# All expert pairs' gated rows split in a high and a low part, normalisations moved to ScalarE, the weights' low parts made on VectorE

## Time and profile before

| | |
|---|---|
| Median of 3 runs | 746.45 us |
| The profiled execution's own time | 748.99 us |
| Its span, first to last instruction | 746.8 us |
| PE busy | 689.9 us (92%), 2943 instructions |
| PE weight loads busy | 516.6 us (69%) |
| DVE busy | 526.0 us (70%), 1070 instructions |
| ACT busy | 350.4 us (47%), 607 instructions |
| POOL busy | 471.0 us (63%), 352 instructions |
| Mean granted TensorE clock | 0.952 |

### The profile page before, as it was taken

How to read it: one execution, slowest core, us unless ns; L and a number is a source line. 1 busy time by engine, 2 the same in 40 slices (tenths; PEclk the granted TensorE clock), 3 DMA queues, 4 the chain that set the end, 5 groups by cost and what they waited for, 6 DMA issues and landing times.

```text
span 746.8 us, 10995 instructions
## 1 busy us (share of the span) xinstructions
PE 689.9 (92%) x2943; PEld 516.6 (69%) x2943; DVE 526.0 (70%) x1070; ACT 350.4 (47%) x607; POOL 471.0 (63%) x352
## 2 busy tenths in 40 slices
PE   4355799999999999989999999999999999999997
PEld 3244577777777767757777777777777777777775
DVE  4846767798678877775777886698777866684443
ACT  3323355534744455523645446544645445543342
POOL 5511657667676757656666766667766656676664
PEclk8555899999999999989999999999999999999999
DMA  5500423333333423333333333334334434335431
GB/s 206 205 1 0 121 85 106 107 110 112 110 100 113 119 88 116 111 99 109 95 107 112 109 111 110 113 82 133 107 100 114 120 93 119 100 112 136 131 123 57
DMA packets 48868, 80.31 MB, mean 108 GB/s; under 512 B 9504, under 2 KB 13728, under 8 KB 48800
## 3 DMA queue, kind: packets, MB, share of 16 engines
q1 hardware_dynamic: 47776, 77.44, 33.9%
q0 software_dynamic: 1024, 2.10, 1.3%
HBM read 76.35 MB, written 3.15 MB: 106 GB/s over the span
## 4 chain that ended last, share of the span: by engine, by line
PE 89%; DVE 5%; issue 2%; ACT 1%; POOL 0%; DVEq 0%; POOLq 0%
PE bank_y L468 15%; PE bank_g L479 8%; PE bank_g L480 8%; PE bank_u L481 8%; PE bank_u L479 8%; PE bank_g L481 8%; PE bank_u L480 8%; PE bank_y L463 4%; PE bank_y L462 4%; PE bank_y L465 4%; PE bank_f L387 1%; PE bank_f L409 1%; PE bank_f L403 1%; PE bank_f L420 1%; PE bank_f L379 1%
## 5 line engine op out<-in xcount | busy, mean ns | idle before, releaser
L1016 POOL TENSOR_TENSOR hid<-hid,gate_rows 128x512 f32<-128x512 f32 x256 | 372.5, 1464 | 195.9 <-DVE hid L855 193.2
L603 ACT ACTIVATE hid<-bank_g 128x512 f32<-128x512 f32 x264 | 156.6, 599 | 279.0 <-PE bank_g L481 268.2
L855 DVE TENSOR_TENSOR hid<-hid,bank_u 128x512 f32<-128x512 f32 x264 | 178.7, 681 | 139.5 <-PE bank_u L481 79.4
L479 PE MATMUL bank_g<-x_hi,gate_hi 128*128 128x512 f32 x264 | 144.1, 546 | 3.7 <-issue 3.7
L468 PE MATMUL bank_y<-hid,w_down 128*128 128x512 f32 x272 | 138.9, 592 | 0.0
L861 DVE TENSOR_TENSOR hid_lo<-hid,hid_hi 128x512 fp32r<-128x512 f32 x128 | 109.5, 855 | 2.6 <-issue 2.2
L480 PE MATMUL bank_g<-x_hi,gate_lo 128*128 128x512 f32 x264 | 105.5, 400 | 0.0
L481 PE MATMUL bank_u<-x_lo,up_hi 128*128 128x512 f32 x264 | 105.4, 399 | 0.0
L479 PE MATMUL bank_u<-x_hi,up_hi 128*128 128x512 f32 x264 | 105.3, 399 | 0.0
L481 PE MATMUL bank_g<-x_lo,gate_hi 128*128 128x512 f32 x264 | 105.2, 399 | 0.0
L480 PE MATMUL bank_u<-x_hi,up_lo 128*128 128x512 f32 x264 | 104.9, 397 | 0.0
(11 more groups left out here) (197 smaller groups left out, 842.7 us busy)
## 6 DMA issues: line engine op xcount, KB each, us to landing
gate_rows<-gates_dram SPq DMA_DIRECT2D x512, 128.0 KB
hid<-gate_t_dram SPq DMA_DIRECT2D x3, 704.0 KB, 7.3
w_down<-down_t_dram SPq DMA_DIRECT2D x3, 704.0 KB, 6.7
out_dram<-later SPq DMA_DIRECT2D x8, 256.0 KB, 2.9
gate_rows<-up_t_dram SPq DMA_DIRECT2D x2, 704.0 KB, 4.9
gates_dram<-gates_t SPq DMA_DIRECT2D x8, 128.0 KB, 2.3
later<-up_t_dram SPq DMA_DIRECT2D x1, 704.0 KB, 8.5
shared<-square_w_dram SPq DMA_DIRECT2D x1, 512.0 KB
```

Of the source, the lines that this page charges most:

```text
L479: pe.matmul(o, w_hi[name][:, p, :], x3_hi[par][:, :], start=True, stop=False)
L603: act.activation(hid[:, slot(par, p), :], bank_g[(p + par) % 2][:, :], ACT.Silu).then_inc(sem("silu"), 1)
L855: dve.tensor_tensor(hid[:, s, :], hid[:, s, :], bank_u[(p + par) % 2][:, :], ALU.mult)\
L1016: pool.tensor_tensor(hid[:, s, :], hid[:, s, :], gate_rows[:, row, :], ALU.mult)\
```

## The change

Every pair, even or odd, goes through `act_hi`, `dve_lo` and three fp32r products; the float32 product of line 468 is gone. The rings `hid_hi` and `hid_lo` have three slots instead of two. `w_down` is split for all pairs, like gate and up, so there are nine chunks instead of six; the late splitting of `down_hi` and `down_lo` is gone. Two buffers of their own are added for staging. All low parts of weights are made on DVE, POOL makes none; three chunks (two of their low parts for steps 22 to 32 of gate and up, one for down) are finished in the first steps of batch 0's loop. `xn`, `x1`, `xn2` and `x3` become ACT instructions that compute scale*x + shift per token; DVE makes only `shift` (minus mean times inverse deviation), a single small instruction for `xn` and `x1` together and one for `x3`.

```diff
-SPLIT_LAG, SPLIT_RING = 2, 2
+SPLIT_LAG, SPLIT_RING = 2, 3
-DVE_AT = dict(xn=0, xn_lo=2, x1=5, xn_dec=5, ..., xn2=11, ..., x3=19, ...
+DVE_AT = dict(shift1=0, xn_lo=2, xn_dec=5, ..., shift3=19, ...
-ACT_AT = dict(xn_hi=2, ...
+ACT_AT = dict(xn=0, x1=3, xn2=11, x3=19, xn_hi=2, ...
-CHUNKS = [(n, p0) for p0 in range(0, PAIRS, CHUNK) for n in ("gate", "up")]
-HI_AT = (-20, -20, -20, -20, 4, 5)
-LO_AT = (("pool", -10), ("vector", 0), ("pool", -10), ("vector", 0), ("pool", 0), ("vector", 6))
+CHUNKS = (("gate", 0, "hid0", None, -20, 3),          # name, first pair, buffer, chunk before it, step of hi, of lo
+          ("up", 0, "hid1", None, -20, 10),
+          ("down", 0, "rows", None, 3, 14),
+          ("up", CHUNK, "later", None, 5, 14),
+          ("down", CHUNK, "own0", None, 5, 22),
+          ("gate", 2 * CHUNK, "own1", None, 7, PAIRS + 5),
+          ("gate", CHUNK, "hid0", 0, 7, 14),
+          ("up", 2 * CHUNK, "later", 3, 22, PAIRS + 7),
+          ("down", 2 * CHUNK, "own0", 4, PAIRS + 8, PAIRS + 10))
...
+            for k, (n, p0, buffer, before, _, _) in enumerate(CHUNKS):      # SP
+                if before is not None:
+                    sp.wait_ge(sem(f"split_lo{before}"), 1)
+                sp.dma_start(raw[buffer], sources[n][:, p0:p0 + CHUNK, :]).then_inc(sem(f"raw{k}"), 16)
...
         def down(pe, b, par, p):
-            if is_split(p):
...
-            else:
-                pe.wait_ge(sem("gated"), q + 1)
-                pe.matmul(y, w_down[:, p, :], hid[:, slot(par, p), :], start=(p == 0),
-                          stop=(p == PAIRS - 1)).then_inc(sem("down_done"), 1)
+            y, k = bank_y[par][:, :], ring_slot(par, p)
+            pe.wait_ge(sem("hid_hi"), q + 1)
+            pe.matmul(y, w_hi["down"][:, p, :], hid_hi[:, k, :], start=(p == 0), stop=False)
+            pe.matmul(y, w_lo["down"][:, p, :], hid_hi[:, k, :], start=False, stop=False)
+            pe.wait_ge(sem("hid_lo"), q + 1)
+            pe.matmul(y, w_hi["down"][:, p, :], hid_lo[:, k, :], start=False,
+                      stop=(p == PAIRS - 1)).then_inc(sem("down_done"), 1)
...
         def act_late(act, b, par, p):
+            for name, k, out in (("xn", 1, xn), ("x1", 0, x1)):
+                if p == ACT_AT[name]:
+                    act.wait_ge(sem("shift1"), b + 1)
+                    for t in range(TILES):
+                        last = act.activation(out[:, t, :], emb[par][:, t, :], ACT.Identity,
+                                              scale=inv1[:, k, t:t + 1], bias=shift1[:, k, t:t + 1])
+                    last.then_inc(sem(name), 1)
+            if p == ACT_AT["xn2"]:
+                act.wait_ge(sem("inv2"), b + 1)
...
+            if p == ACT_AT["x3"]:
+                act.wait_ge(sem("shift3"), b + 1)
...
         def dve_late(dve, b, par, p):
-            if p == DVE_AT["xn"]:
-                dve.wait_ge(sem("inv1"), b + 1)
-                for t in range(TILES):
-                    last = dve.tensor_scalar(xn[:, t, :], emb[par][:, t, :], mv1[:, t, 0:1], inv1[:, 1, t:t + 1],
-                                             ALU.subtract, ALU.mult)
+            if p == DVE_AT["shift1"]:
                 dve.wait_ge(sem("inv1"), b + 1)
+                dve.scalar_tensor_tensor(shift1[:, :, :], mv1[:, :, 0].unsqueeze(1).to_broadcast([P, 2, TILES]), -1.0,
+                                         inv1[:, :, :], ALU.mult, ALU.mult).then_inc(sem("shift1"), 1)
...
         def dve_sequence(dve, b, par, late, early, use=2):
+                if first:
+                    split_lo(dve, PAIRS + p)
                 dve_up(dve, b, par, p)
-                if p >= SPLIT_LAG and is_split(p - SPLIT_LAG):
+                if p >= SPLIT_LAG:
                     dve_lo(dve, b, par, p - SPLIT_LAG)
```

More of the change, by code:

```diff
@@ L46 @@
 LAG = 4
-SPLIT_LAG, SPLIT_RING = 2, 2
-SPLITS = PAIRS // 2
-DOWN_HI_AT, DOWN_LO_AT = 26, 28
+SPLIT_LAG, SPLIT_RING = 2, 3
 GATHER_AT = (1, 2, 3, 4)
-DVE_AT = dict(xn=0, xn_lo=2, x1=5, xn_dec=5, y_lo=4, scores=6, state=6, x2=8, result=10, logits=9, xn2=11, exp_sum=12,
-              h=15, bn1=16, h2=17, bn3=17, mv1=18, x3=19, x3_lo=21, router=24, prob=26, top=27, chosen=28, gates=29,
+DVE_AT = dict(shift1=0, xn_lo=2, xn_dec=5, y_lo=4, scores=6, state=6, x2=8, result=10, logits=9, exp_sum=12,
+              h=15, bn1=16, h2=17, bn3=17, mv1=18, shift3=19, x3_lo=21, router=24, prob=26, top=27, chosen=28, gates=29,
               taken=31)
@@ L119, in build @@
         xn_dec = shared[:, 4 * SEQ:4 * SEQ + (TILES - 1) * P].rearrange("p (t d) -> p t d", t=TILES - 1)
[L121 to L125, removed]
+        w_hi = {n: sb(f"{n}_hi", [P, PAIRS, P], F32R) for n in ("gate", "up", "down")}
+        w_lo = {n: sb(f"{n}_lo", [P, PAIRS, P], F32R) for n in ("gate", "up", "down")}
         ident = sb("ident", [P, P])
@@ L152, in build @@
         inv1 = sb("inv1", [P, 2, TILES])
+        shift1 = sb("shift1", [P, 2, TILES])
+        shift3 = sb("shift3", [P, TILES])
         x1 = sb("x1", [P, TILES, D])
@@ L322, in _ @@
             sp.dma_start(coarse_sb[:, :], coarse_w).then_inc(sem("coarse_w"), 16)
[L323 to L330, removed]
+            sources = {"gate": gate_t, "up": up_t, "down": down_t}
             sp.wait_ge(sem("gathered0"), 16 * TILES)
[L334 to L337, removed]
+            for k, (n, p0, buffer, before, _, _) in enumerate(CHUNKS):
+                if before is not None:
+                    sp.wait_ge(sem(f"split_lo{before}"), 1)
+                sp.dma_start(raw[buffer], sources[n][:, p0:p0 + CHUNK, :]).then_inc(sem(f"raw{k}"), 16)
             store_gates(sp, 0)
@@ L557, in act_late @@
             f0, f1 = bank_f
+            for name, k, out in (("xn", 1, xn), ("x1", 0, x1)):
[7 more added lines that the diff above has]
+                act.wait_ge(sem("inv2"), b + 1)
+                act.wait_ge(sem("xn_dec"), b + 1)
+                for t in range(TILES):
+                    last = act.activation(xn2[:, t, :], x2[:, t, :], ACT.Copy, scale=inv2[:, t:t + 1])
+                last.then_inc(sem("xn2"), 1)
+            if p == ACT_AT["x3"]:
+                act.wait_ge(sem("shift3"), b + 1)
+                for t in range(TILES):
+                    last = act.activation(x3[:, t, :], h2[par][:, t, :], ACT.Identity,
+                                          scale=inv3[:, t:t + 1], bias=shift3[:, t:t + 1])
+                last.then_inc(sem("x3"), 1)
             if p == ACT_AT["xn_hi"]:
@@ L607, in act_hi @@
             act.wait_ge(sem("gated"), q + 1)
-            wait(act, "down_done", q - 2 * SPLIT_RING + 1)
-            act.activation(hid_hi[:, (p // 2) % SPLIT_RING, :], hid[:, slot(par, p), :], ACT.Copy)\
-               .then_inc(sem("hid_hi"), 1)
+            wait(act, "down_done", q - SPLIT_RING + 1)
+            act.activation(hid_hi[:, ring_slot(par, p), :], hid[:, slot(par, p), :], ACT.Copy).then_inc(sem("hid_hi"), 1)
         def act_copy_out(act, b, par):
@@ L716, in dve_late @@
                    .then_inc(sem("x2"), 1)
-            if p == DVE_AT["xn2"]:
-                dve.wait_ge(sem("inv2"), b + 1)
-                for t in range(TILES):
-                    last = dve.tensor_scalar(xn2[:, t, :], x2[:, t, :], inv2[:, t:t + 1], None, ALU.mult)
-                last.then_inc(sem("xn2"), 1)
             if p == DVE_AT["h2"]:
@@ L877, in dve_sequence @@
                     dve_early(dve, b + 2, par, p, use)
+                if first:
+                    split_lo(dve, PAIRS + p)
                 dve_up(dve, b, par, p)
-                if p >= SPLIT_LAG and is_split(p - SPLIT_LAG):
+                if p >= SPLIT_LAG:
                     dve_lo(dve, b, par, p - SPLIT_LAG)
-                elif not first and p < SPLIT_LAG and is_split(p - SPLIT_LAG + PAIRS):
+                elif not first:
                     dve_lo(dve, b - 1, 1 - par, p - SPLIT_LAG + PAIRS)
```

108 lines of the change are left out of this document (41 added, 67 removed).

## The result

The changed kernel takes 787.62 us (median of 4 runs, 784.35 to 789.68), the kernel before 746.32 beside it (745.51 to 747.09): a ratio of 1.055 (95% interval 1.052 to 1.058). The forecast was 731 (710 to 749). The profiled execution has a span of 786.5 us and took 788.29.

A forecast was written before the change was run, and what follows sets the result against it. PE, busy 92% of the span, was taken as the bound, with VectorE nearly level in steps 24 to 33. -21.8 - 9.4 + 12.6 + 2.5 + 2.8 - 2.0 = -15.3 from 748.99 gave 733.7, as median 731 (710 to 749).

The forecast's parts named there:

- PE's gain: Down products of even pairs: 136 fall from 0.86 to 0.70 us each, 21.8 us less on PE.
- the prologue: First 80 us, mostly VectorE's chain: moved normalisations and weight low parts shorten it by 9.4 us, between 5 and 11.
- PE as the only bound: Rival, chance 0.25: low parts find room and PE stays the bound everywhere; 711 us.
- silu of step 0: ScalarE's silu behind xn, which PE needs two steps later: late by no more than xn itself.
- the lateness of the transposes on PE: Transposes of xn (steps 31 to 34) and x3 (step 19): later by 2.5 and 2.8 us over seven batches.
- the scores: Steps after x1 at step 5: x1 leaving VectorE, against low parts of pairs 2 and 4, wins 2.0 us.
- the gates: Steps 24 to 30: three new low parts make the gates 1.8 us late per woven batch, 12.6 us in all.
- the price of a normalisation on ScalarE: Each normalisation on ScalarE takes 0.2 to 0.3 us; four plus the small shift take 1.1 to 1.2.
- VectorE's work: VectorE's total grows by 20 to 40 us; 136 more hid_lo cost 93 to 116, removed normalisations save some 75.
- the small shift: VectorE's small instruction before the normalisation at x3: 0.2 us, or up to 1.4 when it meets POOL.
- The third rival: Chance 0.16: VectorE becomes the bound in steps 24 to 33 and PE's clock falls after gaps; slower, 758 us.
- Theory C: Explanation posed in the experiments: VectorE simply has too much work; it expected 732 us or more for e5.

The follow-up runs named there:

- e4: Changed kernel with each hid_lo replaced by a one-SBUF-input reduction of equal length, leaving out the gated rows' low part: 721.72 us, ratio 0.965.
- e3: Kernel before with only the gate and up weights' low parts moved to VectorE, and the steps of two high parts: 742.73 us, ratio 0.994.
- e15: Changed kernel with x3 alone issued behind silu and hid_hi of step 19: 772.59 us, ratio 1.034.
- e6: Changed kernel with ScalarE's normalisations issued behind silu and hid_hi of their step, except batch 0's: 755.25 us, ratio 1.011.
- e9: Changed kernel with the two shifts made on POOL right behind the inverse deviations: 763.84 us, ratio 1.022.
- e1: Changed kernel with xn, x1, xn2 and x3 back on VectorE: 772.59 us, ratio 1.032.
- e11: Changed kernel with POOL's gathers at steps 1, 3, 5, 7 instead of 1, 2, 3, 4: 770.06 us, ratio 1.031.
- e5: Changed kernel with e4's one-input reduction and e1's normalisations on VectorE: 729.78 us, ratio 0.977.
- e14: Changed kernel with the edits of e6, e9 and e11 together: 737.88 us, ratio 0.987.
- e16: e12 with pairs 10, 12, 14 and 16 split too and four ring slots: 724.48 us, ratio 0.969.
- e12: Kernel before (odd pairs split) with weights' low parts on VectorE in a mended prologue order and gathers at steps 1, 3, 5, 7: 731.52 us, ratio 0.980.

## Why the prediction was wrong

**Right: PE's gain and the prologue.** Three pieces of 0.23 stand for every pair, and in e4 most of the gain is time won (721.7, where 711 was forecast for PE as the only bound). The prologue won 8.0 of the 9.4 forecast, though one of its reasons was wrong: `xn`'s 3.91 us there came from POOL's low parts, not from VectorE. In e3's chain, without them, the same four instructions on VectorE take 1.13 (start us, us, what), less than ScalarE's 1.65.

```profile
20.05 1.13 DVE xn L671 x4
```

The last batch's loop, in which nothing is woven, won 1.6, where its products (17 x 0.16 = 2.7) and a tail of 0 to -1.3 were forecast.

**Failed: "Behind `xn` on ACT stands silu of step 0 ...; it is late by no more than `xn` itself", and the same for `x3`.** I priced the lateness of the transposes on PE (2.5 and 2.8 us) and nothing for the silu behind. But silu feeds VectorE's own next instruction (2.20 idle at steps 19 and 0). With VectorE nearly level with PE, every hold-up of silu is VectorE's; with collisions on the way it does not catch up (in e4 it does), and the delay is carried to the next place where PE needs VectorE: from step 19 to the router (2.05 a loop, e15), from steps 0 and 3 to the scores (1.65 from xn to z and 0.8 from z to state, between e15 and e6). Issuing the same work behind silu gives 32.4 back. PE's waits between 85 and 740 us show where the sum went wrong: 10.0 at step 24 where nothing was put, 8.5 and 5.1 for `xn` and `x3` where 2.5 and 2.8 were, 15.8 at the scores where 2.0 was won; only the gates, 5.8 where 12.6 was put, are below it.

**Mis-sized: the price of a normalisation on ScalarE.** I took 0.2 to 0.3 each from a squaring with no operand per token (299 ns). They take:

```profile
L548 ACT ACTIVATE xn<-emb,shift,inv x32: 477/478/494, 19.9 to 628.4; 128x128 f32<-128x128 f32 x32
```

Four make 1.65 us, not 1.1 to 1.2. The Trainium skill (ScalarE: Activation LUTs, section "What ACT_TABLE_LOAD costs") says that each scale or bias read from a per-partition operand adds some 93 ns; from its figures two of them at 128 columns come to an estimate of 479 ns, and the trace agrees.

**Mis-sized: VectorE's work.** Its total was to grow by 20 to 40 us and grew by 76.7 (526.0 to 602.7). `hid_lo` alone took 134.9 more (109.5 to 244.4), not 93 to 116: its mean rose to 926 ns, above the 855 that was the upper bound.

**Mis-sized: the small shift.** I bounded it at 0.2 to 1.4, saw that 1.4 meant a collision with a product, and took a value near the low end. Its median is 1.248 at both steps: POOL is in a product there. That is 23.8 us with what follows (e9).

**Right in kind: the gates.** From the silu of step 24 to the end of the gates VectorE took 10.96 us before (401.49 to 412.45) and takes 12.47 after (513.56 to 526.03): 1.51 more for three low parts, against 1.8. PE's wait there is 0.84, where 1.8 was forecast; PE is late itself, having waited 1.60 for silu at step 24.

**Wrong sign: the scores.** I put 2.0 won there in all, since `x1` left VectorE, with the low parts of pairs 2 and 4 against it. They lose 2.9 a loop (z to mem, 7.68 to 10.59). In the rows shown, the room that `x1` left (3.23) went to pair 3's low part (3.10 instead of 0.68), which now comes while POOL is still behind its gathers, and these I did not look at. In e1, with `x1` back, pair 3's takes 0.68 in every loop again, but z to mem is 11.00. Gathers apart win 2.7 a loop (e11).

**The third rival was the right one, and too small.** It said that VectorE becomes the bound, through collisions, with the clock paying for gaps of 2 us: 758. It lacked ScalarE's queue and the scores, and it looked for the lost clock in steps 24 to 33: from 100 us on, all the stretches between the scores of one loop and the next ran at 1.00, those steps with them. The clock fell behind the scores alone.

**What stays open.** Theory C is not excluded as a part: 8 us separate e5 from e4. Why e14's gates stretch is 0.75 longer than e6's was not tested; POOL's two shifts, which stand ahead of its products there, are the candidate.

## What to carry to other kernels

Work moved to an engine with idle time is not hidden: ask what stands behind it in that engine's queue, and if that feeds the engine the work was taken from, issue the moved work behind it. Price a collision by the bad case wherever the other engine runs without a break, and look for what puts that engine behind (here gathers in four steps on end). And a product saved on PE is worth making only where the engine that prepares it has room: splitting four more pairs at steps 12 to 18 paid (e16). Splitting all with three mends (e14, 737.9) stays above e12 (731.5), which splits every second pair; splitting all on e12's own kernel was not tried.

## What the runs showed of the hardware

A VectorE instruction with two SBUF inputs that waits for POOL's product does not always get in between that product and the next: `hid_lo` at 457.79 lasted 3.10 us, over two products, and so it did in five loops. Nor does the size of a VectorE instruction bound its wait: the shift on 8 elements per partition took 0.154 us alone and 1.248 beside products. The two sides of a collision show differently: with twice as many `hid_lo` the product's median grew from 1330 to 1677 ns (before, after), while `hid_lo` kept its median (684, 686) and grew a tail.

```profile
L1016 POOL TENSOR_TENSOR hid<-hid,gate_rows x256: 1257/1330/1753, 82.9 to 738.8; 128x512 f32<-128x512 f32 x128
L995 POOL TENSOR_TENSOR hid<-hid,gate_rows x256: 1262/1677/1753, 76.2 to 778.1; 128x512 f32<-128x512 f32 x128
```
